# Batch 0's normalised rows transposed by f32 products with an identity, and a new order of the first three batches

## The chip, the core and the metric

One core of a Trainium2 chip. The metric is the device time of one execution in microseconds; a median of several runs is compared. The kernel has one instruction stream per engine: TensorE (PE, matmul), VectorE (DVE), ScalarE (ACT), GpSimd (POOL) and SyncE (SP, which here only issues DMAs). Each stream runs its own list in order, and the lists meet by semaphores.

## What is computed

A pre-norm attention block and a mixture of experts on eight batches of 512 rows of 256, all f32:

```python
x = x + attn(layernorm(x), Wq, Wk, Wv)      # per batch, causal, one head of 256
x = x + ffn(layernorm(x), ...)              # shared expert + top 2 of 8 routed experts
# attn: softmax(mask(q @ k.T) / 16) @ v,  q = x@Wq, k = x@Wk, v = x@Wv
# ffn:  silu(x@gate.T) * (x@up.T) @ down, inner width 512
#       routing: sigmoid(x@router.T + bias), top 2, weights normalised to sum 1
```

The kernel holds each f32 operand of a product as two f16 parts (high and low) and makes three f16 products (high by high, high by low, low by high; PASSES) that accumulate in f32.

## The kernel before

*Numbers.* B = 8 batches of NB = 4 blocks of P = 128 rows, D = 256 = KD * 128 columns. A "low" part is the f32 value minus its high part.

*Stages.* First the constants, wm = Wq Wk^T (`wm_product`, f32 products), the f16 parts of wm, Wv and the router. Then the batches: the first three in an order written out by hand in each engine's list, batches 3 to 7 by `iteration(i)`, which mixes batch i's attention with batch i-2's shared expert. Then the routed experts, in a loop over groups of two pairs of row blocks, whose results are added to the output by indirect DMA.

*A batch.* DVE takes statistics of the rows (`stats_1`, `aggregate_1`), POOL the power (`rstd1`), DVE the shift (`shift_1`). ACT normalises into xn32 (`xn_normalise`, L762) and casts into xnrow (`xn_high`, L736); the low part is made by POOL (`xn_low`, L564), and for batch 0 by DVE (`first_xn_low`, L1124). SP transposes xnrow into xnt by DMA (`xn_transpose`, L321; batch 1's goes to a part of w). Then TensorE makes T = wm applied to xnt (`t_product`, L1811) and V (`v_product`, L1832), the scores (`scores`, L1855, mask added by L1858), and from the transposed exponentials (`p_transpose`, L345, issued by SP) the attention output (`pv`, L1787). ACT evicts high parts (`t_high`, `v_high`, `p_high`, all L736), DVE the low ones (`t_low`, `v_low`, `p_low`, L1124). The second norm's rows go through xrow and a DMA transpose into xn2t (`xn2_transpose`, L336), then `logits` (L1752), `prefix` (the place of each row in its expert, L1764) and the shared expert (`shared_gate_up` L1711, `shared_down` L1725). POOL scatters the rows to DRAM (`scatter`, L605), after `zero_rows` (L613) has filled that tensor.

*Weights.* All expert weights come in 36 pieces of 384 KB through two buffers, wst: SP loads (`w_load`, L311, waits for the low part of the piece two before), ACT scales and casts (`w_scale`, `w_high`, L736), POOL makes the low part (`w_low`, L581). Until the routed experts begin, only the first four pieces are needed by a product.

*The order.* Nothing but the lists and the waits decides it: an engine whose next step waits holds up all behind it. TensorE's first lines before are

```python
wm_product()
t_product(0, 0, 2)
v_product(0, 0, 2)
scores(0, 0, 4)
```

Before `t_product(0, ...)` it waits for xnt_in (the DMA transpose) and wm_lo. The banks are shared: T uses PT0 and PT1, which also hold the scores of blocks 1 and 2; V uses U[0] and U[1], which the shared expert uses too.

## Time and profile before

| | us |
|---|---|
| median of 3 runs | 576.56 (576.01 to 577.16) |
| the profiled execution | 575.5 |
| its span | 573.7 |
| of which TensorE busy | 519.4 |
| span of the three batches written out | 18 to 87 |
| loop over batches 3 to 7 | from 87 on |
| routed experts | 273 to 541 |

The span runs from the first to the last instruction that the profiler saw; 1.8 us of the execution lie around it. TensorE's profile has two rows for a product: PEld is the load of the stationary operand, PE the product. An f32 product appears as two of each. The ends of products are modelled, so the starts are the better guide; a group's time is from the start of its first to the end of its last.

### The profile page before, as it was taken

Reading aid. Unit: us, or ns where it says so; the run is one execution under the profiler, and the core shown is the slowest. Engines: PE = TensorE matmul, PEld = TensorE weight load, DVE = VectorE, ACT = ScalarE, POOL = GpSimd, SP = SyncE. Lnnn points to the kernel's source line nnn. Section 1 sums busy time; section 2 is a strip of 40 time slices with the busy share of each in tenths; the row PEclk is TensorE's granted clock in tenths of the full one; section 3 lists DMA queues with packets and bytes.
Section 4 is the critical chain, followed back from the end, with each engine's and each line's share of the span. In section 5 each row is a group of like instructions: output and inputs, shape, how many; then the busy total and the mean of one; then the engine's idle time right before and its main releaser. Section 6 shows DMA issues by size and latency. Waiting matters only on the chain.

```text
span 573.7 us, 14737 instructions
## 1 busy us (share of the span) xinstructions
PE 519.4 (91%) x4521; PEld 422.1 (74%) x4522; DVE 372.4 (65%) x933; ACT 306.6 (53%) x578; POOL 288.4 (50%) x236
## 2 busy tenths in 40 slices
PE   2778899898989999896999999999999999999980
PEld 1455688686777878775688888788888888888870
DVE  5468999878897978899455455545455554555440
ACT  4979888686767566652243443444444434444440
POOL 3653788676685856766014534434344434344433
PEclk9999999999999999999899999999999999999995
DMA  7898876949493939652636554565655556445542
GB/s 259 219 199 151 155 183 128 256 108 206 134 208 112 201 134 174 178 151 77 139 59 103 82 78 77 84 86 75 90 84 75 82 86 89 76 74 76 82 56 27
DMA packets 147546, 70.45 MB, mean 123 GB/s; under 512 B 122384, under 2 KB 140560, under 8 KB 147504
## 3 DMA queue, kind: packets, MB, share of 16 engines
q1 hardware_dynamic: 133904, 50.69, 42.4%
q0 software_dynamic: 13600, 19.22, 19.3%
q8 instruction: 24, 0.39, 0.3%
q14 instruction: 18, 0.15, 0.1%
HBM read 19.48 MB, written 23.54 MB: 75 GB/s over the span
## 4 chain that ended last, share of the span: by engine, by line
PE 58%; SPq 12%; DMA 10%; DVE 10%; issue 4%; ACT 3%; POOL 2%; POOLq 0%; ACTq 0%; DVEq 0%
PE bank L1711 27%; PE bank L1725 15%; PE bank L1984 6%; SPq L336 4%; DMA wst<-w_all 4%; SPq L345 4%; DMA ptr<-phl 3%; PE bank L1999 3%; SPq L321 2%; PE bank L1832 2%; PE bank L1787 2%; PE bank L1811 2%; PE bank L1855 1%; DMA out<-p,wm 1%; DMA out<-tt,wm 1%
## 5 line engine op out<-in xcount | busy, mean ns | idle before, releaser
L1711 PE MATMUL bank<-xn2t,w 128*128 128x256 f16 x1728 | 197.2, 273 | 0.9 <-DVE th L1298 0.8
L1711 PEld LDWEIGHTS bank<-xn2t,w 128*128 (+1 forms) x1728 | 168.5, 98 | 24.5 <-DVE th L1298 1.4
L691 POOL DMA_INDIRECT out<-p,wm x56 | 87.4, 1561 | 117.1 <-issue 55.0
L1289 DVE SCALAR_TENSOR_TENSOR th<-th,bank 128x512 f32<-128x512 f32 x88 | 60.1, 682 | 71.5 <-ACT th L780 71.4
L1725 PE MATMUL bank<-w,h 128*128 (+1 forms) x864 | 101.3, 273 | 3.0 <-DVE z L1221 2.0
L1725 PEld LDWEIGHTS bank<-w,h 128*128 128x128 f16 x864 | 83.5, 98 | 15.3 <-DVE z L1221 3.2
L736 ACT ACTIVATE h<-th 128x512 f16<-128x512 f32 x72 | 45.2, 628 | 87.0 <-DVE th L1298 85.1
L780 ACT ACTIVATE th<-bank 128x512 f32<-128x512 f32 x88 | 52.4, 596 | 46.9 <-PE bank L1711 46.7
L1124 DVE TENSOR_TENSOR h<-th,h 128x512 f16<-128x512 f32 x72 | 49.8, 692 | 39.2 <-ACT h L736 39.1
L581 POOL TENSOR_TENSOR w<-wst,w 128x768 f16<-128x768 f32 x36 | 59.3, 1649 | 26.3 <-ACT w L736 26.0
L605 POOL DMA_INDIRECT rows<-xrow,sidx x56 | 57.2, 1022 | 27.1 <-DVE sidx L1281 15.3
L1298 DVE SCALAR_TENSOR_TENSOR th<-th,bank 128x512 f32<-128x512 f32 x88 | 60.1, 682 | 2.2
L691 POOL DMA_INDIRECT out<-tt,wm x15 | 24.0, 1597 | 69.8 <-DMA out<-p,wm 39.2
L1984 PE MATMUL bank<-w,ptr 128*128 x180 | 41.3, 379 | 0.0
L1061 ACT ACTIVATE p<-bank,wm 128x256 f32<-128x256 f32 x56 | 23.6, 471 | 23.3 <-issue 13.2
L1787 PE MATMUL bank<-v,ptr 128*128 128x256 f16 x240 | 29.9, 273 | 6.4 <-DMA ptr<-phl 6.4
L736 ACT ACTIVATE wst<-wst 128x768 f32<-128x768 f32 x36 | 29.9, 834 | 8.4 <-DMA wst<-w_all 8.3
L1811 PE MATMUL bank<-xnt,wm 128*128 128x512 f16 x84 | 21.7, 402 | 11.9 <-DVE wm L1125 7.7
L1711 PE MATMUL bank<-w 128*128 128x256 f16 x288 | 32.4, 273 | 0.0
L1787 PEld LDWEIGHTS bank<-v,ptr 128*128 128x128 f16 x240 | 22.3, 98 | 12.2 <-DMA ptr<-phl 9.1
L1984 PEld LDWEIGHTS bank<-w,ptr 128*128 128x128 f16 x180 | 17.6, 98 | 18.2 <-issue 0.3
L736 ACT ACTIVATE w<-wst 128x768 f16<-128x768 f32 x36 | 30.3, 841 | 0.7
(156 smaller groups left out, 710.0 us busy)
## 6 DMA issues: line engine op xcount, KB each, us to landing
wst<-w_all SPq DMA_DIRECT2D x36, 384.0 KB
x<-x SPq DMA_DIRECT2D x8, 512.0 KB, 5.6
out<-x SPq DMA_DIRECT2D x8, 512.0 KB, 4.9
rows<-xrow POOLq DMA_DIRECT2D x1, 1192.5 KB, 7.4
rows<-xrow,sidx POOLq DMA_INDIRECT x56
out<-p,wm POOLq DMA_INDIRECT x56, 4.0
wm<-rows SPq DMA_DIRECT2D x28, 9.0 KB, 1.9
xn2t<-rows SPq DMA_TRANSPOSE x28, 3.7
```

The source lines that it names most:

```text
L581: cc.tensor_tensor(w_ap(j, 1, c * CH, CH), wst[:, (g % 2) * CH:(g % 2 + 1) * CH], w_ap(j, 0, c * CH, CH), ALU.subtract).then_inc(w_lo, 1)
L605: cc.indirect_dma_start(rows, bass.IndirectOffsetOnAxis(ap=sidx_of(b)[:, m:m + 1], axis=0), xrow[b % 2][:, n * RW:(n + 1) * RW].bitcast(I3 ...
L691: cc.indirect_dma_start(out, bass.IndirectOffsetOnAxis(ap=index, axis=0), part, None, compute_op=ALU.add).then_inc(y_out, 16)
L736: return a.activation(o, i, ACT.Copy, scale=scale)
L780: a.activation(th[:, half * 512:(half + 1) * 512], G[half][:, :], ACT.Tanh, scale=0.5 / WS).then_inc(f_tanh, 1)
L1124: return d.tensor_tensor(o, full, hi, ALU.subtract)
L1289: d.scalar_tensor_tensor(out=tb, in0=tb, scalar=1.0, in1=G[half][:, :], op0=ALU.add, op1=ALU.mult).then_inc(f_sg, 1)
L1298: d.scalar_tensor_tensor(out=tb, in0=tb, scalar=0.5 / (WS * WS), in1=U[half][:, :], op0=ALU.mult, op1=ALU.mult).then_inc(f_h, 1)
L1711: ins = mm(dst, w_ap(j, ws, m * MAT + k * I + (2 * half + i) * P, P), moving(ms * KD + k), start=(cnt == 0), stop=(cnt == 3 * KD - 1))
L1725: ins = mm(o[:, a * D:(a + 1) * D], hb[:, (hs * KI + i) * TT + a * P:(hs * KI + i) * TT + (a + 1) * P], w_ap(j, ws, 2 * MAT + i * D, D), s ...
L1787: ins = mm(PV_BANK[q // 2][:, (q % 2) * D:(q % 2 + 1) * D], ptr[:, off + (ps * (q + 1) + kb) * P:off + (ps * (q + 1) + kb + 1) * P], v[:, ...
L1984: ins = mm(o[:, :], xs_t[:, c * P:(c + 1) * P], w_ap(j, ws, m * MAT + kk * I, I), start=(cnt == 0), stop=(cnt == 3 * KD - 1))
```

## The change

Batch 0's normalised rows are no longer cast, split and transposed by DMA. ACT normalises blocks 0 and 1, DVE blocks 2 and 3 (`first_xn_normalise`). TensorE multiplies each 128x128 block of xn32, as the stationary operand, by an f32 identity (`first_transposes`, eight products of 128 columns into PT1 and PT2). ACT casts the two banks into the high half of xnt, DVE subtracts into the low half (`first_xn_high`, `first_xn_low`). The identity is made by POOL in the spare part of w. Batch 0's transpose leaves SP's list, and the counts of xn_lo, xn_hi and xnt_in go down by one batch for all others. The semaphore xn2t_in becomes two, by parity of the batch.

All five lists of the first three batches have a new order. The loop, the tail and the routed experts are as before.

```diff
+        ident32 = spare[:, 4144:4144 + 2 * P].bitcast(F32)
...
+        XN_BANK = (PT1, PT2)
+        xnt4 = xnt[:, :].rearrange("p (n c r) -> p n c r", n=NB, r=P)
...
@@ SP
             x_load(1)
             x_load(2)
+            w_load(0)
             x_load(3)
-            w_load(0)
             w_load(1)
-            xn_transpose(0)
...
             w_load(2)
+            xn_transpose(1)
             w_load(3)
-            xn_transpose(1)
+            x_load(4)
             w_load(4)
-            x_load(4)
             p_transpose(0, 0)
             p_transpose(0, 1)
             p_transpose(0, 2)
-            w_load(5)
             p_transpose(0, 3)
             xn_transpose(2)
+            w_load(5)
             w_load(6)
...
@@ POOL
+            const(cc.memset(ident32, 0.0))
...
+            const(cc.affine_select(out=ident32, in_=ident32, compare_op=ALU.not_equal, fill=1.0,
+                                   base=0, pattern=[[-1, P]], channel_multiplier=1))
...
             rstd1(0)
             rstd1(1)
             w_low(0)
+            xn_low(1)
             w_low(1)
+            w_low(2)
             rstd1(2)
+            xn_low(2)
             zero_rows()
-            xn_low(1)
-            w_low(2)
             w_low(3)
-            xn_low(2)
...
-            scatter(0, 0, 2)
             w_low(8)
-            scatter(0, 2, 5)
+            scatter(0, 0, 5)
             w_low(9)
...
@@ ACT
+            def first_xn_high(k):
+
+                act.wait_ge(xn0_mm, 2)
+                copy(xnt4[:, :, k, :], bank3(XN_BANK[k])).then_inc(xn0_hi, 1)
...
             router_high()
+            xn_normalise(0)
             wv_high()
-            xn_normalise(0)
-            xn_high(0)
+            wm_high()
             w_scale(0)
+            first_xn_high(0)
+            first_xn_high(1)
+            w_scale(1)
             w_high(0)
-            w_scale(1)
-            w_high(1)
-            wm_high()
             xn_normalise(1)
             xn_high(1)
+            v_high(0, 0)
+            t_high(0, 0)
+            t_high(0, 1)
+            w_high(1)
...
@@ DVE
+            def first_xn_normalise():
+
+                dve.wait_ge(shift1, 1)
+                for i in (2, 3):
+                    ins = d.tensor_scalar(xn32[:, i * D:(i + 1) * D], x1[:, i * D:(i + 1) * D], rstd[0][:, i:i + 1],
+                                          nmr[:, i:i + 1], ALU.mult, ALU.add)
+                ins.then_inc(xn0_dve, 1)
+
+            def first_xn_low(k):
+
+                dve.wait_ge(xn0_hi, k + 1)
+                low(xnt4[:, :, KD + k, :], bank3(XN_BANK[k]), xnt4[:, :, k, :]).then_inc(xn0_lo, 1)
...
@@ TensorE
+            def first_transposes(h):
+
+                pe.wait_ge((xn_put, xn0_dve)[h], 1)
+                for n in (2 * h, 2 * h + 1):
+                    for k in range(KD):
+                        ins = mm(XN_BANK[k][:, n * P:(n + 1) * P], xn32[:, n * D + k * P:n * D + (k + 1) * P],
+                                 ident32, start=True, stop=True)
+                ins.then_inc(xn0_mm, 1)
...
             wm_product()
-            t_product(0, 0, 2)
-            v_product(0, 0, 2)
+            first_transposes(0)
+            first_transposes(1)
+            t_product(0, 0, 1)
+            v_product(0, 0, 1)
+            t_product(0, 1, 2)
+            v_product(0, 1, 2)
             scores(0, 0, 4)
+            t_product(1, 0, 1)
             v_product(1, 0, 1)
-            t_product(1, 0, 2)
+            t_product(1, 1, 2)
             pv(0, 0, 1)
             v_product(1, 1, 2)
-            pv(0, 1, 3)
-            scores(1, 0, 2)
+            pv(0, 1, 2)
+            scores(1, 0, 1)
+            pv(0, 2, 3)
+            scores(1, 1, 2)
             pv(0, 3, 4)
             scores(1, 2, 4)
             t_product(2, 0, 2)
-            pv(1, 0, 2)
             v_product(2, 0, 1)
-            pv(1, 2, 4)
+            pv(1, 0, 4)
             v_product(2, 1, 2)
-            scores(2, 0, 3)
+            scores(2, 0, 4)
             logits(0)
             shared_gate_up(0, 0)
-            scores(2, 3, 4)
             prefix(0)
...
```

## Rows read from the trace of the kernel before

**Rows 1.** The page's part 1: busy us, share of the span, instructions.
```profile
PE 519.4 (91%) x4521; PEld 422.1 (74%) x4522; DVE 372.4 (65%) x933; ACT 306.6 (53%) x578; POOL 288.4 (50%) x236
```

**Rows 2.** Windows: stretch, length, then busy us (instructions) of each engine.
```profile
18.00:87.00 69.00, 61.62 (x527) 45.58 (x528) 56.59 (x196) 58.56 (x116) 44.08 (x36) 1.00 0.87 182
87.00:242.00 155.00, 145.40 (x1351) 117.87 (x1349) 133.07 (x405) 109.04 (x213) 106.35 (x91) 1.00 0.71 166
```

**Rows 3.** Timeline, first 19 us: start, length, engine, line, count [idle before, releaser].
```profile
6.34 1.05 POOL L551 TENSOR_TENSOR rstd<-ve,halves 128x4 f32<-128x4 f32 x1 [2.64 <-DVE ve L1144]
6.62 3.78 PE L1688 MATMUL bank<-v 128*128 128x256 f32 x8 [6.62 <-DMA v<-wk_t]
8.47 2.06 ACT L762 ACTIVATE xn<-x,nmr,rstd 128x256 f32<-128x256 f32 x4
12.90 2.04 SPq L321 DMA_TRANSPOSE xnt<-xnrow  x1
16.70 0.58 ACT L736 ACTIVATE wm<-bank 128x512 f16<-128x512 f32 x1
17.31 0.69 DVE L1125 SCALAR_TENSOR_TENSOR wm<-bank,wm 128x512 f16<-128x512 f32 x1 [3.04 <-ACT wm L736]
18.11 0.14 PEld L1811 LDWEIGHTS bank<-xnt,wm 128*128 128x128 f16 x2 [8.43 <-DMA xnt<-xnrow]
18.14 4.37 PE L1811 MATMUL bank<-xnt,wm 128*128 128x512 f16 x12 [7.74 <-DVE wm L1125]
```

**Rows 4.** One line's or tile's instructions, to 40 us: ns min/median/max, first and last start.
```profile
L1688 PEld LDWEIGHTS bank<-v x8: 288/337/337, 6.6 to 9.3; 128*128 128x128 f32 x8
L1811 PEld LDWEIGHTS bank<-xnt,wm x12: 97/147/147, 18.1 to 21.9; 128*128 128x128 f16 x12
```

**Rows 5.** Timeline of TensorE, 18 to 87 us: the products that serve as checkpoints.
```profile
24.96 0.50 PE L1855 MATMUL bank<-xnt,tt 128*128 128x128 f16 x6
...
29.35 1.48 PE L1832 MATMUL bank<-wvs,w 128*128 128x256 f16 x12 [0.74 <-DMA w<-xnrow]
...
40.09 1.48 PE L1787 MATMUL bank<-v,ptr 128*128 128x256 f16 x12 [2.30 <-DMA ptr<-phl]
...
42.74 1.47 PE L1855 MATMUL bank<-w,tt 128*128 128x512 f16 x6
...
45.77 2.75 PE L1811 MATMUL bank<-xnt,wm 128*128 128x512 f16 x12 [1.50 <-DVE w L1124]
...
55.05 0.50 PE L1855 MATMUL bank<-xnt,tt 128*128 128x128 f16 x6
...
58.81 2.78 PE L1711 MATMUL bank<-xn2t,w 128*128 128x256 f16 x24
...
86.66 0.50 PE L1855 MATMUL bank<-xnt,tt 128*128 128x128 f16 x6
```

**Rows 6.** Timeline of DVE and POOL: two DVE steps beside POOL's subtraction.
```profile
32.05 2.13 POOL L564 TENSOR_TENSOR xnrow<-xn,xnrow 128x1024 f16<-128x1024 f32 x1 [2.08 <-ACT xnrow L736]
32.07 2.13 DVE L1144 TENSOR_SCALAR ve<-mv 128x4 f32<-128x4 f32 x1
...
61.20 2.13 POOL L564 TENSOR_TENSOR xnrow<-xn,xnrow 128x1024 f16<-128x1024 f32 x1
61.70 1.65 DVE L1238 CAST idxf<-ix 128x8 f32<-128x8 uint32 x1
```

**Rows 7.** Chain that ended last, two pieces: start, length, what.
```profile
35.09 4.95 DMA ptr<-phl
...
63.87 5.67 DMA xnt<-xnrow
```

**Rows 8.** Groups by line, 18 to 87 us: busy us, mean ns.
```profile
L736 ACT ACTIVATE w<-wst 128x768 f16<-128x768 f32 x11 | 9.2, 838 | 0.1
L581 POOL TENSOR_TENSOR w<-wst,w 128x768 f16<-128x768 f32 x11 | 18.3, 1664 | 4.1 <-ACT w L736 3.9
```

**Rows 9.** Timeline of TensorE at the start of the routed experts.
```profile
273.12 4.87 PE L1725 MATMUL bank<-w,p 128*128 128x256 f16 x24 [5.42 <-DVE p L1124]
```

More of the change, by code:

```diff
@@ L388, in _ @@
             p_transpose(1, 1)
[L389 removed]
             p_transpose(1, 2)
             p_transpose(1, 3)
[L392 removed]
+            w_load(7)
             xn2_transpose(0, 0)
@@ L656, in _ @@
             w_low(11)
+            put_idx(1)
             rstd2(2)
```

251 lines of the change are left out of this document (128 added, 123 removed).

## Prediction

> **What bounds the kernel now.** I read the page's busy shares first, then busy time by stage, then TensorE's timeline, then the other engines only where TensorE waits. The shares [rows 1] name TensorE as the engine to watch (91%). The stages [rows 2] say where it is not full: from 18 to 87 (batches 0 to 2, written out by hand) it works 61.62 of 69 and so idles 7.4, and in the loop over batches 3 to 7 it idles 9.6 in 155. In the first 18 us it works 3.78 [rows 3]. The loop's own order is not edited. So what the change is worth is what it does to the time at which the loop's first product starts, 86.66 us [rows 5], provided that the rest follows rigidly.
>
> What ends the long first wait? Two things, at nearly the same time [rows 3]: the low part of wm (16.70 to 17.28 on ACT, to 18.00 on DVE), and batch 0's DMA transpose, issued 12.90, for which the first weight load waited to 18.11; the first product starts at 18.14. Moving either one alone would give almost nothing. wm is late only because ACT's list puts four weight pieces and batch 0's rows ahead of it: its product had ended at 10.40. The change removes both causes. A second thing to see is the clock: batch 0's twelve 512-column products fill 4.37 us [rows 3], batch 2's twelve 2.75 [rows 5], and of their weight loads most take 147 ns, the fastest, at 21.9, 97 [rows 4]. TensorE is at its lower level (1.2 GHz) there, after 7.7 us of idling, and rises to 2.4 GHz only about 3.8 us into the burst.
>
> **The change, part by part.**
>
> *Constants.* A memset and an affine_select of a 128x128 f32 identity on POOL. The 16-bit ones are 0.2 to 0.3 us; even at twice that, 1.1 us together, they fit in the 2.64 us that POOL idles before the first rstd [rows 3]. Cost nothing; without that cover up to 1.1.
>
> *Normalising batch 0.* ACT does two of four blocks (2.06/2 = 1.03, about 8.05 to 9.1), DVE the other two. A DVE form of this is not in the trace; for 256 columns I bound it by 0.17 (small tensor_scalar) and 0.5 (512 columns take 0.69), done by 8.7. TensorE is in wm's product until 10.40, which hides both.
>
> *The transposes.* Eight f32 products of 128 columns, two records each: 16. From below: wm's eight records of 256 columns took 3.78, half of that per record is 0.236, sixteen make 3.8. From above: a f32 weight load is 337 ns [rows 4]; if it binds, 5.4; if load and product don't overlap at all, 0.337 + 0.213 each, 8.8. At the higher clock throughout about half of the first, 2 us. I take 3.8, because TensorE then runs unbroken from 6.62 on and should rise to the upper level on the way. So the transposes end at 10.4 + 3.8 = 14.2 (range 12.4 to 19.2).
>
> The Trainium skill (TensorE: Matmul & The Clock Gate, "Weight-path perf modes") says fast weight load is off for f32; the trace agrees (337 against 147 ns at the same clock).
>
> *Eviction.* Two ACT copies (0.58, as wm's) and two DVE subtractions (0.69), pipelined: 0.1 + 0.58 + 0.69 + 0.60 + 0.1 = 2.1. First product at 16.3: 1.8 us earlier. wm_low now ends about 12.5 and is no longer a condition. TensorE idles only 2.1 us before it, so I expect the higher clock: another 1.6 us (4.37 less 2.75).
>
> *What this becomes in the new order.* I walked the lists of all engines with the trace's durations: an ACT weight piece 0.84 twice and POOL's part of it 1.66 [rows 8], xn_low 2.13 [rows 6], 512 columns 0.58 on ACT and 0.69 on DVE, less 0.1 where the next follows without a wait; TensorE 1.3 per half product. Checkpoints, before [rows 5] against the walk:
> - scores of batch 0: 24.96 to 22.3. Products end at 21.5, but ACT has two weight halves, batch 1's normalise and cast between: it, not TensorE, sets the 22.3.
> - first product of batch 1: 29.35 to 27.9. Here the gain shrinks to 1.4. Batch 1's rows still go by DMA: cast 19.9, POOL's subtraction 22.1 (in place of 23.8), then 5.3 us to land (12.90 to the load at 18.11; 5.67 later [rows 7]). T's bank is also held until p_low(0,1), about 27.4 to 28.1. TensorE idles 2.2 us where it idled 0.7.
> - last scores of batch 1: 42.74 to 38.9. The P transpose of the last block is issued at 32.1 instead of 35.09, because before a DVE step was stuck 2.13 us [rows 6]; the 2.30 us wait at 40.09 nearly goes.
> - T of batch 2: 45.77 to 42.5, new wait 2.2 (p_low(1,1), and batch 2's transpose beside the 1.2 MB zeroing of the rows, which POOL now issues later).
> - scores of batch 2: 55.05 to 52.1. The P transposes 2 and 3 of batch 1, issued to 45.6, bind.
> - shared gate/up 0: 58.81 to 56.9, with 1.3 us of scores done ahead: 3.2 in all.
> - then the prefix stands right behind gate/up half 0 and waits for the router's mask, about 1.8 us; before, scores of block 3 stood between.
> - from there TensorE is nearly full: the loop starts at 84.3 against 86.66.
> Sum: 1.8 (start) + 1.6 (clock) - 1.0 (net new idle) = 2.4. The walk leaves out small semaphore gaps; I take 2.2.
>
> *Moved steps.* On SP, w_load(0) passes x_load(3): the first piece comes sooner, the fourth x is needed at 29. One transpose issue (2.04) is gone. w_load(5) and (7) come after the P transposes: the pieces are used by ACT at 42.6 and 50.5, half a dozen us later than they can land. On POOL, scatter(0) takes five in a row ahead of w_low(9), some 6 us, which only delays weights that the loop's list takes later. put_idx(1) is 0.2. On ACT and DVE the reordered steps are in the walk. Splitting xn2's semaphore costs nothing: each consumer waits for the same landing.
>
> **What can take it back.** In the trace a DVE step on SBUF data that starts while POOL runs ends with POOL's instruction: 2.13 beside 2.13, and the cast of the router's indices 1.65 [rows 6]. Aggregates, bias rows and casts meet other POOL steps in the new order; the walk has two such meetings, 1.5 and 1.1 us. The Trainium skill (SBUF — State Buffer, on the shared port pair) calls this an exclusive lock for the whole instruction; the trace agrees. Which meetings occur can't be read from the lists to 0.1 us. Further on, the loop's waits are on transposes and DVE, and TensorE's 5.42 us wait before 273.12 [rows 9] ends with DVE's table: all of these move with the start, each worth some tenths either way.
>
> **Rivals.**
> 1. *Absorbed.* Two more meetings of DVE and POOL on the chain, or 1.5 us more at the mask. For: DVE is busy 56.6 of 69 us in this stage [rows 2]. Against: the old order had them too. Left: 0 to 1.1 us; about 575.9.
> 2. *The clock stays low through batch 0's products.* They end about 1.9 us later, 23.6, T's low half about 24.9, scores 25.0, so 2.7 of the gain go: 576.9. For: the gap of 2.1 us, and f32 products of 128 columns may leave the array half idle. Against: the idle stretch of 2.30 us before 40.09 is followed by full-speed products (1.48 for twelve of 256 columns) [rows 5].
> The Trainium skill (TensorE: Matmul & The Clock Gate, "Part 4: PE-mode transpose") says that the upper clock doesn't engage for transpose-mode products. These are plain f32 products, so I don't expect it to apply; by it the time would be this rival's. No row here shows such products.
> 3. *Slower: the transposes don't overlap their weight loads.* 8.8 us, ending 19.2: the whole chain over ACT starts 5.0 later, so 2.2 becomes -2.8: 579.4. It decides from 0.38 us a record (6.0 us in all, end at 16.4) on; slower by 0.2% from 0.45. For: 337 ns loads ahead of products of only 128 columns, eight different blocks. Against: in wm's product [rows 3] eight records of 634 ns fill 3.78 us, so they do overlap.
> 4. *More.* The order removes idle time that my walk still has (2.2 and 2.2 before T of batches 1 and 2, 1.8 at the mask) and the transposes run at the upper clock: 4.2 us, 572.4.
>
> **The numbers.** The profiled execution took 575.5 (span 573.7 and 1.8 around it); the median of the runs is 576.56, 1.06 above it. 575.5 - 2.2 = 573.3, on the scale of the median 574.4. About 0.2% (1.15 us) is what a measurement of this kernel can tell from no change. Forecast (gain 1.15 to 3.4): 0.42, its own range 573.2 to 575.4. More: 0.13. Absorbed: 0.20. Low clock: 0.10. Slower: 0.15. Faster 0.55, same 0.30, slower 0.15. The range leaves out most of the slower case and the far end of the fourth: 572.2 to 577.6.
>
> **What would show it.** In the profile after: f32 products of 128 columns between 10.4 and about 14.2; first 512-column product at about 16.3 with 97 ns weight loads; scores of batch 0 at 22.3, first product of batch 1 at 27.9 released by the DMA or DVE's p; last scores of batch 1 near 39; T of batch 2 near 42.5; a wait for the mask of 1 to 2 us; loop from 84.3, and 31 us an iteration as before. The prediction is wrong if the transposes take over 6 us, if batch 1's transposed rows land after 29.3, or if the loop starts early and the end doesn't move with it.

## The result: slower by 0.7 %

The changed kernel took 580.87 us (median of 4 runs, 580.49 to 582.48) beside 576.28 us for the kernel before (median of 4, 575.52 to 577.16): 1.0072 times, 95 % interval 1.0041 to 1.0103. Forecast were 574.4 us and "faster". Two later measurements, on other chips, gave 1.0091 (1.0052 to 1.0129) and 1.0069 (1.0041 to 1.0096). The profiled execution took 582.48 us, its span was 580.6 us, against 575.5 and 573.7. It is the slowest of its four and the one before is the fastest of its four, so the two spans differ by 6.9 us where the medians differ by 4.6.

First the page of the profile after, part 1 (busy us, share of the span, instructions), as [rows 1].

```profile
span 580.6 us, 14775 instructions
PE 524.4 (90%) x4537; PEld 426.2 (73%) x4538; DVE 376.6 (65%) x936; ACT 305.1 (53%) x577; POOL 289.2 (50%) x238
```

TensorE's work grew by 5.0 us, of which the transposes are 2.2; the products are otherwise the same ones. Two groups alone, T of batch 2 and gate/up 0, took 3.9 us more below, at the lower clock, and T of batch 0 took 1.4 us less. The windows of the changed kernel show where (stretch, length, busy us of PE, PEld, DVE, ACT and POOL with their instructions, PEclk, DMA share, GB/s), as [rows 2].

```profile
0.00:18.00 18.00, 8.65 (x44) 6.80 (x46) 9.80 (x35) 8.74 (x16) 6.46 (x23) 1.00 0.65 212
18.00:87.00 69.00, 55.55 (x455) 40.31 (x454) 55.09 (x180) 52.54 (x108) 40.64 (x32) 0.93 0.84 171
87.00:242.00 155.00, 145.80 (x1359) 118.71 (x1357) 133.34 (x406) 110.51 (x213) 104.77 (x91) 1.00 0.70 166
```

From 18 to 87 us TensorE works 55.55 us where it worked 61.62, and its mean clock is 0.93. From 87 to 242 us it is as busy as it was (145.80 against 145.40). So most of the result lies ahead of the loop; the table has the share. TensorE's timeline after, at the checkpoints of [rows 3] and [rows 5]:

```profile
10.21 2.16 PE L1750 MATMUL bank<-w,xn 128*128 128x128 f32 x16
15.08 1.47 PE L1850 MATMUL bank<-xnt,wm 128*128 128x512 f16 x6 [2.71 <-DVE xnt L1144]
...
21.67 0.51 PE L1895 MATMUL bank<-xnt,tt 128*128 128x128 f16 x6 [1.21 <-DVE tt L1144]
...
27.22 1.46 PE L1850 MATMUL bank<-w,wm 128*128 128x512 f16 x6 [1.89 <-DVE w L1144]
...
41.22 1.47 PE L1895 MATMUL bank<-w,tt 128*128 128x512 f16 x6 [1.66 <-DVE x L1410]
45.36 4.14 PE L1850 MATMUL bank<-xnt,wm 128*128 128x512 f16 x12 [2.62 <-DMA xnt<-xnrow]
...
55.23 0.50 PE L1895 MATMUL bank<-xnt,tt 128*128 128x128 f16 x6
...
62.98 5.28 PE L1740 MATMUL bank<-xn2t,w 128*128 128x256 f16 x24 [3.52 <-DVE v L1144]
68.05 0.23 PE L1802 MATMUL bank<-mask,tri 128*128 128x32 f16 x1
...
92.23 0.50 PE L1895 MATMUL bank<-xnt,tt 128*128 128x128 f16 x6
```

| first product of | before [rows 3, 5] | forecast | after | after less before |
|---|---|---|---|---|
| T of batch 0 | 18.14 | 16.3 | 15.08 | -3.1 |
| scores of batch 0 | 24.96 | 22.3 | 21.67 | -3.3 |
| batch 1 (before V, after T) | 29.35 | 27.9 | 27.22 | -2.1 |
| last scores of batch 1 | 42.74 | 38.9 | 41.22 | -1.5 |
| T of batch 2 | 45.77 | 42.5 | 45.36 | -0.4 |
| scores of batch 2 | 55.05 | 52.1 | 55.23 | +0.2 |
| shared gate/up 0 | 58.81 | 56.9 | 62.98 | +4.2 |
| loop | 86.66 | 84.3 | 92.23 | +5.6 |

The part of the change that is its point worked better than forecast: 3.3 us were gained by 21.67. Then they were lost: 1.2 us up to batch 1, as forecast, 2.3 between there and the scores of batch 2, 4.0 more up to gate/up 0, and 1.4 on the way to the loop. Of the 4.0, 1.3 us are not lost time but the scores of block 3, which stood behind gate/up 0 before and stand ahead of it now; so the stretch from there to the loop loses 2.7 us and not 1.4, and 2.5 of these are the slow gate/up products themselves (5.28 us against 2.78). From the loop's first scores to the end of the span are 487.0 us before and 488.4 after, so 1.4 of the 6.9 us of span come behind the loop's start.

### The profile page after: what moved, and what is told of

It is laid out like the page before. It is cut to its first block, busy times and chain, and to the rows that moved or that the text cites. A ratio compares the mean times of both kernels' runs of the same rounds, so it can differ in the third digit from the quotient of the medians.

```text
span 580.6 us, 14775 instructions
## 1 busy us (share of the span) xinstructions
PE 524.4 (90%) x4537; PEld 426.2 (73%) x4538; DVE 376.6 (65%) x936; ACT 305.1 (53%) x577; POOL 289.2 (50%) x238
## 4 chain that ended last, share of the span: by engine, by line
PE 54%; SPq 12%; DMA 11%; DVE 9%; issue 5%; ACT 4%; POOL 3%; POOLq 0%; ACTq 0%; DVEq 0%
PE bank L1740 26%; PE bank L1763 14%; PE bank L2032 6%; DMA wst<-w_all 5%; SPq L344 4%; DMA ptr<-phl 4%; SPq L353 4%; PE bank L2047 3%; SPq L329 2%; PE bank L1872 1%; DMA out<-tt,wm 1%; DMA out<-p,wm 1%; DVE th L1327 1%; PE bank L1825 1%; SPq L319 1%
## 5 line engine op out<-in xcount | busy, mean ns | idle before, releaser
L1740 PE MATMUL bank<-xn2t,w 128*128 128x256 f16 x1728 | 200.0, 275 | 4.6 <-DVE v L1144 3.5
L703 POOL DMA_INDIRECT out<-tt,wm x15 | 25.2, 1679 | 71.4 <-DMA out<-p,wm 40.5
L1825 PEld LDWEIGHTS bank<-v,ptr 128*128 128x128 f16 x240 | 22.4, 98 | 11.5 <-DMA ptr<-phl 7.3
L1740 PEld LDWEIGHTS bank<-w 128*128 128x128 f16 x288 | 27.9, 98 | 3.7
## 6 DMA issues: line engine op xcount, KB each, us to landing
rows<-xrow POOLq DMA_DIRECT2D x1, 1192.5 KB, 10.5
```

What stands on the lines that cost most here:

```text
L703: cc.indirect_dma_start(out, bass.IndirectOffsetOnAxis(ap=index, axis=0), part, None, compute_op=ALU.add).then_inc(y_out, 16)
L1740: ins = mm(dst, w_ap(j, ws, m * MAT + k * I + (2 * half + i) * P, P), moving(ms * KD + k), start=(cnt == 0), stop=(cnt == 3 * KD - 1))
L1825: ins = mm(PV_BANK[q // 2][:, (q % 2) * D:(q % 2 + 1) * D], ptr[:, off + (ps * (q + 1) + kb) * P:off + (ps * (q + 1) + kb + 1) * P], v[:, ...
```

## Where the start was lost, read from the trace after

**Between 34 and 45 us.** DVE, POOL and SP's queue, in that order (start, length, engine, line, operation, count):

```profile
36.79 2.81 DVE L1164 TENSOR_SCALAR ve<-mv 128x4 f32<-128x4 f32 x1
```

```profile
35.01 1.28 POOL L626 DMA_DIRECT2D rows<-xrow  x1
36.32 3.25 POOL L594 TENSOR_TENSOR w<-wst,w 128x768 f16<-128x768 f32 x2
```

```profile
35.16 2.29 SPq L329 DMA_TRANSPOSE xnt<-xnrow  x1
38.00 2.36 SPq L319 DMA_DIRECT2D wst<-w_all  x2
```

A four-element step of DVE, ve of batch 3, takes 2.81 us (0.17 when POOL is idle): it starts while POOL splits two weight pieces back to back (36.32 to 39.57), and ends with the second. Behind it stand the row maximum of the next scores and the additions that free TensorE's bank, so TensorE waits 1.66 us at 41.22. At the same time POOL issues the 1.2 MB zeroing of the rows 0.15 us before SP issues batch 2's transpose. The transposed rows are used at 45.36, 10.2 us after their issue; in [rows 3] batch 0's took 5.2. In the view of DMA issues (KB each, median us to landing) the zeroing takes 10.5 us to land; it was 7.4 before:

```profile
rows<-xrow POOLq DMA_DIRECT2D x1, 1192.5 KB, 10.5
```

**Between 57 and 68 us.** The timeline of ACT, then POOL, then DVE:

```profile
54.72 0.84 ACT L748 ACTIVATE wst<-wst 128x768 f32<-128x768 f32 x1 [1.27 <-DMA wst<-w_all]
55.47 2.06 ACT L776 ACTIVATE xn<-x,nmr,rstd 128x256 f32<-128x256 f32 x4
```

```profile
57.68 1.98 POOL L564 TENSOR_TENSOR rstd<-ve,halves 128x4 f32<-128x4 f32 x2 [2.37 <-ACT xn L776]
59.64 2.11 POOL L577 TENSOR_TENSOR xnrow<-xn,xnrow 128x1024 f16<-128x1024 f32 x1
```

```profile
58.72 0.16 DVE L1169 SCALAR_TENSOR_TENSOR nmr<-mv,rstd 128x4 f32<-128x4 f32 x1 [0.95 <-POOL rstd L564]
...
59.70 2.08 DVE L1169 SCALAR_TENSOR_TENSOR nmr<-mv,rstd 128x4 f32<-128x4 f32 x1 [0.75 <-POOL rstd L564]
...
62.16 0.67 DVE L1144 TENSOR_TENSOR v<-bank,v 128x512 f16<-128x512 f32 x1
...
65.39 1.22 DVE L1267 CAST idxf<-ix 128x8 f32<-128x8 uint32 x1
...
66.90 0.19 DVE L1271 TENSOR_TENSOR mask<-one_hot 128x32 f16<-128x32 f32 x1
```

ACT waits 1.27 us for a weight piece, so its normalising of batch 3 ends at 57.5; POOL's rstd of batch 4 has to wait for that and holds rstd of batch 1's second norm behind it; both shifts of DVE wait for POOL (0.95 and 0.75), and the second, a step of 0.16 us, then lies 2.08 us beside POOL's subtraction. v_low(2,0), which frees the bank of gate/up 0, stood ahead of all this in the old order and stands behind it in the new one. TensorE idles 3.52 us and then runs its 24 products in 5.28 us instead of 2.78. Windows of 1 us of the same stretch (stretch, length, PE, PEld, DVE, ACT, POOL, PEclk, DMA share, GB/s):

```profile
62.00:63.00 1.00, 0.02 (x1) 0.05 (x2) 1.00 (x5) 1.00 (x3) 0.00 (x0) 0.50 0.00 1
...
67.00:68.00 1.00, 1.00 (x6) 0.75 (x5) 1.00 (x3) 0.94 (x2) 0.98 (x1) 0.50 0.48 99
68.00:69.00 1.00, 1.00 (x13) 0.79 (x11) 0.90 (x8) 0.70 (x2) 0.15 (x1) 0.67 0.40 60
```

So a chain of waits can be read. Whether each of them costs what it seems to is another question; the rest of this section's reading was put to the chip.

## Experiments

The experiments ran on other chips than the result, and the kernel before took 577.8 to 582.8 us there; so ratios are compared, each with the kernel before measured beside it. The scatter is larger than in the first measurement, and intervals of about ±0.3 % are what it allows. Between groups of measurements ratios carry over roughly: the changed kernel had 1.0069 to 1.0091 in three, the transposes alone 1.0047 and 1.0080 in two. One group is to be read with more care. On one and the same chip (14) the kernel before took 577.75 us beside new_order_dma, front_new and score_shift and 582.78 beside after_third, 0.9 % more, while the variants had medians of 585.7 to 587.7 us in the first group and 586.1 to 589.4 in the second. The three ratios of 1.015 and above are all of the first group, which had no changed kernel in it, and may owe a part of that to the kernel before.

### One wait at a time

`v_first`: v_low(2,0) ahead of the waiting shifts.

```diff
             row_max(2, 1)
-            shift_1(4)
             minus_max(2, 1)
+            v_low(2, 0)
+            shift_1(4)
             shift_2(1)
             row_max(2, 2)
-            v_low(2, 0)
```

> One line of DVE's list moved: batch 2's V subtraction stands before shift_1(4) and shift_2(1) instead of behind them. Theory A (the 3.52 us wait ahead of the first gate/up product, and the clock that falls after it): the wait goes, the 24 products take 2.8 us instead of 5.3, the loop starts 4 to 6 us earlier than 92.2, time 575 to 577. Rival B (something else is late just behind it, a transpose or the mask): the wait moves to the prefix or to T of batch 3 and the loop starts less than 2 us earlier, time above 579. Rival C (the loss sits in the loop or the tail, not here): the loop starts earlier and the time stays at 581.

`filler`: thirty products whose result nobody reads, to keep TensorE busy in its wait.

```diff
             logits(0)
+            filler(30)
             shared_gate_up(0, 0)
```

> The changed kernel plus 30 products of 256 columns into a bank that the next product overwrites, put into the wait ahead of the first gate/up product (their results are not used). The wait stays as long as it was. If half of the loss there is the clock, the 24 gate/up products take 2.8 us instead of 5.3 and the time is about 2.5 us below 580.9, 578.4. If the slow products have another cause (operands, memory), they stay at 5.3 us and the time stays at 581 or above.

`agg_early`: the DVE step that got stuck for 2.81 us goes elsewhere.

```diff
             v_low(0, 1)
+            aggregate_1(3)
             p_low(0, 3)
...
-            aggregate_1(3)
```

> One line of DVE's list moved: aggregate_1(3) stands before p_low(0,3), where POOL is idle, instead of where POOL makes two weight pieces. Theory A: its 2.81 us step shrinks to 0.17, the last scores of batch 1 start at about 39.5 instead of 41.2, but T of batch 2 waits for its DMA transpose (45.3) anyway, so the time moves by less than 1 us. Rival: the stuck step delays everything behind it on DVE and the gain of 2 us or more reaches the loop, time 579 or less.

`zero_early`: the zeroing ahead of batch 2's rows.

```diff
             rstd1(2)
+            zero_rows()
             xn_low(2)
-            zero_rows()
```

> One line of POOL's list moved: the 1.2 MB zeroing of the rows is issued before batch 2's subtraction (at about 26.5, where POOL idles 6.6 us) instead of just behind it, so it no longer runs beside batch 2's DMA transpose. Theory A: the transpose takes 5 to 6 us instead of 10, T of batch 2 starts at about 43.5 instead of 45.4 and at the upper clock (2.8 us instead of 4.1), but batch 0's P transposes get later by 1 to 3 us; net 0 to 3 us faster than 580.9. Rival: the transpose's 10 us have another cause (weight loads in the same queue), T of batch 2 still starts after 45, time 581 or more.

| kernel | ratio (95 %) | T of batch 2: start, length, wait | gate/up 0 | loop |
|---|---|---|---|---|
| the change, result | 1.0072 (1.0041 to 1.0103) | 45.36, 4.14, 2.62 for the transpose | 62.98, 5.28, 3.52 for DVE | 92.23 |
| the change, after_again | 1.0091 (1.0052 to 1.0129) | 46.74, 4.45, 2.77 for the transpose | 63.16, 2.78, 2.00 for DVE | 95.89 |
| the change, after_third | 1.0069 (1.0041 to 1.0096) | 48.68, 4.45, 3.55 for the transpose | 65.11, 4.45, 2.02 for DVE | 98.89 |
| v_first | 1.0096 (1.0063 to 1.0129) | 48.36, 4.45, 3.25 for DVE | 62.63, 2.78, no wait | 94.57 |
| filler | 1.0090 (1.0057 to 1.0123) | 47.69, 4.23 | 65.23, 2.78 | 95.32 |
| agg_early | 1.0104 (1.0046 to 1.0162) | 48.57, 5.30, 5.90 for the transpose | 65.91, 2.78, 2.00 for DVE | 98.17 |
| zero_early | 1.0088 (1.0055 to 1.0120) | 49.05, 4.44, 2.09 for DVE | 66.69, 4.45, 3.25 for DVE | 96.96 |

The first three rows are one and the same kernel: its own profiles differ by 3.3 us at T of batch 2 and by 6.7 at the loop, so that starts of single profiles can't be compared to a us or two; which wait is there and which isn't can. None of the four variants is faster than the change by more than the error. Each took away what it was meant to and met the next: v_first has no wait at gate/up 0, and 3.62 us at the prefix, for the mask; agg_early has no stuck step, and 5.90 us for the DMA transpose that ran beside the zeroing; zero_early let that transpose land in time and put the zeroing beside the transposes of batch 0's P. In filler gate/up 0 ran at full speed (2.78) and the ratio stayed; but it ran at full speed in after_again too, without any filler, behind a wait of 2.00 us. So filler shows that a full clock at gate/up 0 doesn't bring the time back, and not that the filler is what kept it.

### Several, and the parts alone

`after_again` is the changed kernel once more, as it is. `shift_late` takes both shifts out of each other's way; `three_moves` adds agg_early and zero_early.

```diff
-            rstd1(4)
             rstd2(1)
+            rstd1(4)
             xn_low(3)
...
             row_max(2, 1)
-            shift_1(4)
             minus_max(2, 1)
...
             ffn_low(0, 1)
+            shift_1(4)
             p_low(2, 3)
```

> The changed kernel unaltered, so that the variants sent with it have it on the same chip. 0.7 to 1.0% above the kernel before, with the waits of its first profile: about 3.5 us before the first gate/up product and slow products behind it.

> The changed kernel with batch 4's shift put back behind ffn_low(0,1) on DVE and batch 1's second rstd put back ahead of batch 4's on POOL. v_first showed that the wait only moved from the first gate/up product to the mask, so DVE is what is late there. Theory D (DVE is held up some 3.6 us between 58 and 62 by waiting for two rstd and by 2.0 us of nmr stuck beside xn_low(3)): both the wait before gate/up and the one before the prefix shrink to under 1.5 us, the products run at the upper clock, the loop starts 4 us or more earlier, 3 to 5 us faster than after_again. Rival (DVE is simply full, the order of these two steps doesn't matter): under 1 us faster.

> shift_late with the moves of agg_early and zero_early as well. Alone, each of the two only uncovered the other: with the aggregate early T of batch 2 waited 5.9 us for its DMA transpose, with the zeroing early it waited for p_low(1,1) behind the stuck aggregate. If they are one wait with two holders, both together start T of batch 2 about 2 us earlier than after_again, at the upper clock, and the time is 1 to 3 us below shift_late. If a third thing holds it, it equals shift_late within 0.5 us.

Measured: after_again 1.0091 (1.0052 to 1.0129), shift_late 1.0081 (1.0048 to 1.0115), three_moves 1.0075 (1.0044 to 1.0107). The ratio of after_again was as expected, the wait was not: 2.00 us before gate/up 0 and full speed behind it, where 3.5 us and slow products were expected. None of the three can be told from the others by its time. In shift_late gate/up 0 starts at 59.62 without a wait, 3.4 us earlier than in the result, but the loop at 93.06. TensorE's timeline of shift_late, and DVE's:

```profile
65.41 0.19 PE L1802 MATMUL bank<-mask,tri 128*128 128x32 f16 x1 [3.01 <-DVE mask L1271]
...
66.10 4.13 PE L1740 MATMUL bank<-xn2t,w 128*128 128x256 f16 x24 [0.38 <-DVE v L1144]
```

```profile
60.54 0.79 DVE L1257 TENSOR_SCALAR pr<-ez 128x32 f32<-128x32 f32 x1
...
62.84 1.15 DVE L1267 CAST idxf<-ix 128x8 f32<-128x8 uint32 x1
64.03 1.10 DVE L1269 TENSOR_TENSOR one_hot<-eidx,idxf 128x64 f32<-128x64 f32 x1
65.16 0.19 DVE L1271 TENSOR_TENSOR mask<-one_hot 128x32 f16<-128x32 f32 x1
```

The wait has gone one place on, to the mask, whose chain on DVE meets POOL three times (0.16 to 0.23 us of work each where POOL is idle), and with the wait the clock falls there (4.13).

`transposes_old_order`, twice, the second as `transposes_again`: the products with the identity, with the lists of the kernel before on all engines, except that on ACT xn_normalise(0) stands ahead of wv_high, wm_high behind it, and the copies of batch 0's rows behind w_scale(0), and that on DVE wm_low stands ahead of the copies' low parts. `new_order_dma` is the converse: the new lists, with batch 0's rows cast, split and transposed by DMA as before.

> The f32 transposes alone: all lists in the old order but for the steps that they need (wm's high part right behind its product, the two evictions, batch 0's transpose gone from SP). Theory D (the loss is the new order's, the transposes gain): first product at 15 to 15.5, loop start 84 to 86 against 86.7, 0 to 3 us faster than the kernel before. Rival E (the early start itself costs, because every later step is bound by DMA and DVE, which gain nothing): the loop starts at 86.7 or later, time equal to before or slower.

> The transposes alone in the old lists once more (transposes_old_order), beside the kernel before and after on one chip. Theory: by themselves they start TensorE 1.5 us earlier and the rest takes it back, ratio 1.000 to 1.005; if it is again 1.004 to 1.006 with an interval above 1.001, the transposes too cost something (scores of batch 0 wait for ACT's copy of T behind four weight pieces: 4 us in the first run).

> The new order alone: the lists of the changed kernel, but batch 0's rows go by the DMA transpose as before (cast on ACT, low part on DVE, issue on SP behind w_load(1)). Theory 'the new order is what costs': the first product at about 18, checkpoints to 43 about 1 to 2 us later than in the changed kernel, and at the loop nearly as late: 587 to 588, ratio 1.009 to 1.011. Rival 'the transposes cost as much as the order': ratio 1.004, 584 to 585.

Measured: transposes alone 1.0047 (1.0012 to 1.0081) and 1.0080 (1.0049 to 1.0110); new order alone 1.0149 (1.0117 to 1.0182). Against the kernel before measured beside it, the order alone costs, clearly, and more than its theory said (1.009 to 1.011). Whether it costs more than order and transposes together (1.0069 to 1.0091) is not clear: by its median (585.68 us, against 586.49 for after_third on the same chip) new_order_dma is no slower. The transposes alone cost too, as rival E had it (loop at 93.23 and 91.25, not at 84 to 86), and TensorE's timeline of transposes_again shows where the first of it is lost:

```profile
10.05 2.65 PE L1753 MATMUL bank<-w,xn 128*128 128x128 f32 x16
16.06 5.30 PE L1853 MATMUL bank<-xnt,wm 128*128 128x512 f16 x12 [3.36 <-DVE xnt L1145]
...
27.18 0.51 PE L1898 MATMUL bank<-xnt,tt 128*128 128x128 f16 x6 [2.94 <-DVE tt L1145]
```

T's products end at 21.4 and ACT has copied both halves by 24.2; DVE is what is late, as its timeline and POOL's show:

```profile
21.05 4.88 DVE L1170 SCALAR_TENSOR_TENSOR nmr<-mv,rstd 128x4 f32<-128x4 f32 x1
25.85 1.27 DVE L1145 TENSOR_TENSOR tt<-bank,tt 128x512 f16<-128x512 f32 x2
```

```profile
20.86 1.28 POOL L626 DMA_DIRECT2D rows<-xrow  x1
22.17 2.14 POOL L577 TENSOR_TENSOR xnrow<-xn,xnrow 128x1024 f16<-128x1024 f32 x1
24.26 1.63 POOL L594 TENSOR_TENSOR w<-wst,w 128x768 f16<-128x768 f32 x1
```

A step of 0.15 us is held for 4.88 us, from POOL's issue of the zeroing through two further instructions, until POOL pauses at 25.89; in transposes_old_order it is held for 4.88 us as well. In before_again, the kernel before on the same chip, the same step starts 0.14 us into the same issue and is through in 0.14:

```profile
20.76 0.14 DVE L1149 SCALAR_TENSOR_TENSOR nmr<-mv,rstd 128x4 f32<-128x4 f32 x1
```

Here it starts 0.19 us into it. This meeting puts the scores of batch 0 at 27.18, not at 25.73 as in before_again (below), and the 1.5 us are still there at gate/up 0 (60.59 against 59.10). It is 2.3 us at T of batch 3, for whose transpose TensorE waits 1.49 us against 0.72, and 3.2 at the loop (91.25 against 88.07), so about half of the lateness comes later. No run took the meeting away by itself; its price of 1.5 us is a reading of two profiles on one chip.

### The new front on the old rest

`before_again` is the kernel before, profiled beside these. `front_new` has the new lists up to the last scores of batch 1 and the old ones from T of batch 2 on, but with the zeroing ahead of xn_low(2). `score_shift` is shift_late with the scores of block 3 back ahead of the prefix.

```diff
-            scores(2, 0, 4)
+            scores(2, 0, 3)
             logits(0)
             shared_gate_up(0, 0)
+            scores(2, 3, 4)
             prefix(0)
```

> The kernel before, unchanged, as the yardstick: a profile of it taken on the same chip as the others. Expected about 582 us, ratio 1.000. The theories use its checkpoints: T of batch 2 at about 45.8, shared gate/up 0 at 58.8, loop start at 86.7, each perhaps 0.5 to 1 us later than in the first profile.

> The changed kernel up to the last scores of batch 1 (transposes by products, new lists of all five engines, but the zeroing of the rows ahead of xn_low of batch 2 and the aggregate of batch 3 early, as before), and from T of batch 2 on every engine's list as in the kernel before. Theory 'the gain is made in batches 0 and 1 and lost between 43 and 69 by the new order there': last scores of batch 1 some 1 to 1.5 us earlier than before, gate/up 0 at about 57 to 58 and the loop 1 to 2 us earlier than in the kernel before: 580 to 581, ratio 0.997 to 0.999. Rival 'whatever starts early waits later, because DVE and the transposes set the pace from 30 on': the loop starts where it did, ratio 1.000 +/- 0.002. Rival 'the new front itself costs something later (weights later, the clock)': like the changed kernel, 586 to 587, ratio 1.008.

> The changed kernel with shift_late's two moves (shift_1(4) behind ffn_low(0,1) on DVE, rstd2(1) ahead of rstd1(4) on POOL) and with scores(2,3) behind gate/up half 0, ahead of the prefix, as in the kernel before. Theory 'the prefix's wait for the mask (3.0 us in shift_late) and the fall of the clock behind it are the loss once gate/up is on time': the wait shrinks by the 1.3 us of scores and the second half of gate/up runs at 2.78 instead of 4.1 to 4.5: loop 1.5 to 2.8 us earlier than in shift_late, 585, ratio 1.003 to 1.005. Rival 'DVE's and the transposes' pace sets the loop's start': the wait only moves to the scores or the later products, ratio 1.008.

Measured: before_again 1.0022 (0.9999 to 1.0046), which is the same kernel on both sides, so 0.2 % is what such a ratio can be off by, loop at 88.07; score_shift 1.0150 (1.0121 to 1.0178), and the prefix still waits 3.23 us for the mask although 1.4 us of scores stand in front of it; front_new 1.0178 (1.0140 to 1.0216), the highest ratio of all. That is what the third rival of front_new's expectation says, and score_shift lies above both of its theories. My theory for front_new was wrong as the kernel was made, and ACT's and SP's timelines show the mistake:

```profile
46.25 0.84 ACT L749 ACTIVATE wst<-wst 128x768 f32<-128x768 f32 x1 [8.25 <-DMA wst<-w_all]
```

```profile
31.18 5.26 SPq L353 DMA_TRANSPOSE ptr<-phl  x2
...
40.29 1.94 SPq L329 DMA_TRANSPOSE xnt<-xnrow  x1
```

The zeroing, issued at 28.18, ran beside batch 0's P transposes (two issues take 5.26 us; TensorE waited 3.71 us for one of them), and w_load(5) stood behind batch 2's transpose in SP's queue, so ACT, whose list was the old one there, idled 8.25 us. A joint between lists has to fit on five engines at once.

> The changed kernel, unchanged, as the yardstick for the other three on the same chip. Expected 1.008 to 1.015 times the kernel before (585 to 587 us).

> The changed kernel with the zeroing store issued by POOL right behind w_low(0), at about 18 us, and aggregate_1(3) ahead of p_low(0,3). Theory (a), the zeroing's place is the loss: no DMA transpose behind batch 1's rows runs beside it, batch 2's rows land in 5 us instead of 10, T of batch 2 starts at 43 to 44 (45.4 to 46.7 in the changed kernel), the loop 2 to 4 us earlier, ratio 1.002 to 1.006. Rival (b), the lists from batch 2 on: T of batch 2 earlier, but gate/up 0 or the prefix wait that much longer, loop no more than 1 us earlier than in the changed kernel. Third: batch 1's own transposes are the ones that now run beside it, first product of batch 1 at 31 instead of 27 to 28, and nothing is gained.

> New front up to batch 1's last scores, the old lists from T of batch 2 on (as front_new), with front_new's two faults mended: the zeroing store at about 18 us instead of 28, and w_load(5) ahead of the last P transpose as in the kernel before. Theory: the 8.3 us wait of ACT for weights and the 3.7 us of TensorE for P go, and the early start is kept: loop 1 us earlier to 1 us later than in the kernel before, ratio 0.998 to 1.003. Rival, the front's gain can't be carried past 45 whatever the lists: 1.005 or more.

Measured: after_third 1.0069 (1.0041 to 1.0096), zero18_agg 1.0106 (1.0059 to 1.0152), front_mended 1.0099 (1.0070 to 1.0128). Zeroing at 18 us frees batch 2's transpose (T of batch 2 at 44.88, 48.68 in after_third) but now runs beside batch 1's, whose first product waits 3.12 us (28.41): the third case of its expectation. In front_mended w_load(5), ahead of the last P transpose, waits in SP's queue for POOL's third weight piece, which the new front finishes only at 39.6; the P transpose behind it is issued at 39.98 and TensorE waits 4.63 us for it. The two theories stayed undecided, but after_third showed the size of the first suspect: ve of batch 3 starts in POOL's issue of the zeroing, at 37.62, and is held to 41.99, where the second of the two weight pieces behind it ends.

```profile
37.62 4.37 DVE L1164 TENSOR_SCALAR ve<-mv 128x4 f32<-128x4 f32 x1
```

It was 2.81 us in the profile of the result, 2.60 in shift_late, 4.12 in after_again, 4.37 in new_order_dma and 4.38 in score_shift. The kernels whose aggregate_1(3) or zeroing is elsewhere (three_moves, zero18_agg, zero13_all, front_new, front_good) have no held step above 2.1 us.

`zero13_all`: the changed kernel with the zeroing where no transpose is on its way, and the moves of agg_early and shift_late. `front_good`: the new lists of all engines up to about 45 us (DVE's up to the scores of batch 1), with that zeroing and aggregate_1(3) moved likewise; from there the old lists.

```diff
             rstd1(1)
+            zero_rows()
             w_low(0)
...
             xn_low(2)
-            zero_rows()
             w_low(3)
```

> The changed kernel with three waits taken away together: the zeroing store at about 13 us, aggregate_1(3) ahead of p_low(0,3) on DVE, and shift_1(4) behind ffn_low(0,1) with rstd2(1) ahead of rstd1(4). Theory, these three are the loss: T of batch 2 at 43 to 45, gate/up 0 at 57 to 59, and the mask's wait of 1.5 to 3 us is what remains: loop at 89 to 90.5, ratio 1.003 to 1.005. Rival, DVE's and POOL's meetings in the mask's chain take it back: loop at 92 to 94 as in shift_late and three_moves, ratio 1.007 to 1.010.

> New front up to batch 1's last scores with its own weight loads and ACT steps, the zeroing store issued at about 13 us (before w_low(0)), aggregate_1(3) ahead of p_low(0,3), and the old lists of PE, DVE, POOL and ACT from T of batch 2 on. Theory, the lists of batch 2 lose the gain: scores of batch 1 at 35 to 36, T of batch 2 at 43 to 44.5, gate/up 0 at 57 to 59, loop 0.5 to 2 us earlier than in the kernel before (85 to 87.5), ratio 0.997 to 1.000. Rival, the gain of the front can't be carried whatever the lists, because ACT's weight pieces that the front puts off come due there: loop at 89 or later, ratio 1.004 or more.

Measured together: **zero13_all 583.01 us, 1.0012 (0.9985 to 1.0040)**; **front_good 579.97 us, 0.9955 (0.9931 to 0.9979)**, beside 581.88 us for the kernel before. front_good beats both kernels. Its time is better than its theory said (0.997 to 1.000) although its loop starts later (88.72 against 85 to 87.5), and the same goes for zero13_all (1.003 to 1.005; loop at 89 to 90.5). TensorE's timeline of front_good, then POOL's and the landing of the zeroing:

```profile
15.95 2.74 PE L1853 MATMUL bank<-xnt,wm 128*128 128x512 f16 x6 [3.07 <-DVE xnt L1145]
...
43.95 2.75 PE L1853 MATMUL bank<-xnt,wm 128*128 128x512 f16 x12 [1.50 <-DVE w L1145]
...
57.66 2.78 PE L1743 MATMUL bank<-xn2t,w 128*128 128x256 f16 x24
...
63.45 0.19 PE L1805 MATMUL bank<-mask,tri 128*128 128x32 f16 x1 [1.66 <-DVE mask L1272]
...
63.59 5.40 PE L1743 MATMUL bank<-xn2t,w 128*128 128x256 f16 x48
```

```profile
13.43 1.28 POOL L626 DMA_DIRECT2D rows<-xrow  x1
```

```profile
rows<-xrow POOLq DMA_DIRECT2D x1, 1192.5 KB, 7.7
```

T of batch 2 runs at 43.95 in 2.75 us, gate/up 0 at 57.66 in 2.78, and no wait of TensorE between 34 and 70 us exceeds 1.7 us. In zero13_all gate/up 0 is as early (58.03), and the mask's wait of 3.01 us, with 4.41 us for the half product behind it, remains: its loop starts at 91.31, front_good's at 88.72.

**What follows.** zero13_all, the changed kernel without the three waits that were read from the trace, is as fast as the kernel before (1.0012), while the changed kernel had 1.0069 to 1.0091. That is about 0.6 %, but between groups of measurements: the changed kernel was not measured beside zero13_all. So the three moves together probably remove most of the loss; how much each of them does is not shown. The place of the zeroing on POOL is common to most of the waits: it lengthens transposes, and POOL's run of instructions behind it holds DVE. three_moves and zero13_all differ in nothing but that place (27 against 13 us) and measured 1.0075 and 1.0012, again on different chips. A rival stands untested: that the zeroing at 13 us would do it alone. It was tried at 27 (zero_early) and at 18 (zero18_agg), each time beside other transposes, and never at 13 without the other moves.

The new order from there on costs 3.0 us more (583.01 less 579.97, same chip, measured together). front_good as a whole gains 1.9 us on the kernel before by the medians, 2.6 by the ratio. How much of that is the transposes by products is not shown: front_good also has the zeroing 7 us earlier and new lists for the first two batches, and neither the kernel before with the early zeroing nor front_good with batch 0's rows by DMA was measured. Open too is in which stretch front_good keeps its gain. Its profile, one execution on another chip than before_again's, has gate/up 0 at 57.66 against 59.10 but the loop at 88.72 against 88.07; the times, not the two profiles, show the gain.

## Why the prediction was wrong, step by step

- *Constants, normalising on DVE: right.* DVE's two blocks took 0.73 us, within the 0.34 to 1.0 given.
- *Transposes: over-sized, in the safe direction.* 16 records in 2.16 us, not 3.8 (1.95 to 3.17 in the other runs). The rate of the wm product, 0.236 us for 128 columns, didn't carry over. Rival 3 (8.8 us) was far off.
- *Eviction and first product: right.* 2.71 us of idle against 2.1, start at 15.08 against 16.3. The clock held in this profile (1.47 us for six products). In others with the same first products it didn't, and the length of the idle stretch doesn't sort them: 2.74 us for the six after 2.27 (filler), 2.65 (score_shift), 2.79 (zero13_all), 2.97 (after_third) and 3.07 (front_good), but 1.47 after 2.73 (zero18_agg) and 1.51 after 3.70 (after_again). So "TensorE idles only 2.1 us before it, so I expect the higher clock" came true by luck as much as by reason. Rival 2 thus comes and goes. What it costs at the scores of batch 0 runs from next to nothing (21.77 in zero13_all against 21.64 in zero18_agg) to 2.7 us (24.35 in front_good against 21.67), and front_good has none of it left at the last scores of batch 1 (40.92 against 41.22). The price on record for this rival is also mis-added: 574.4 and 2.7 are 577.1, not 576.9. The Trainium skill (TensorE: Matmul & The Clock Gate, "Part 4: PE-mode transpose") says the upper clock doesn't engage for transpose-mode products; behind these plain f32 products the next six took 1.47 us, which is the upper level, so nothing of the kind is seen for them in the result, and no run here has transpose-mode products.
- *The clock in the first 20 us is read from lengths.* The prediction puts TensorE at the lower level at 18.14 in the kernel before, by 4.37 us for twelve products and 147 ns weight loads. The granted clock of the same stretch reads 1.00 in the profile before, from 18 to 23 us. The two don't agree, and the lengths are what the prediction's reading rests on.
- *Batch 1: right up to 28 us* (27.22 against 27.9, wait 1.89 against 2.2), *then wrong.* "Last scores at 38.9" failed on the size of one term: the meetings of DVE with POOL. The walk had two, of 1.5 and 1.1 us. The real ones ahead of the loop are 1.27, 2.81, 2.08, 1.22 and 1.25 us, and the second is over 4 us in later runs: a step is held until POOL pauses, not until its instruction ends, so 1.65 or 2.13 [rows 6] is no upper bound. The prediction said itself that these meetings can't be read from the lists; the consequence, a wider range upward, was not drawn. By the last scores of batch 1 the forecast was missed by 2.3 us. The held step is about 1.4 of what was missed: from the first scores of batch 0 to the last of batch 1 the result takes 19.55 us, agg_early and zero13_all without that step 18.05 and 18.16, the walk 16.6. Which step took the rest is not shown. The Trainium skill (SBUF — State Buffer, "Who interferes with whom") has the lock for a whole instruction; the holds of 2.81 to 4.88 us, over two and three instructions, are longer than that.
- *T of batch 2 at 42.5: wrong by 2.9 us.* The zeroing was named, but priced inside a 2.2 us wait, with 5.3 us for the transpose. Beside the zeroing it took 10.2. And the clock fell in the 2.62 us wait (4.14 instead of 2.75). I had argued against that from one row: full speed behind 2.30 us of idling [rows 5]. That is no bound: in after_third the clock fell behind 2.02 us (gate/up 0, 4.45).
- *Gate/up 0 at 56.9: wrong by 6.1 us, the largest miss.* The dependence was left out of the walk: rstd of batch 4 waits for ACT's normalising of batch 3, holds the next rstd behind it on POOL, and shift_1(4), moved from behind ffn_low(0,1) to ahead of v_low(2,0), hands that wait to TensorE. The prediction says of the reordered steps that they "are in the walk"; a step moved forward past an important one needs its own release time looked up. This is the step of the prediction that failed by most: the path from the scores of batch 2 to gate/up 0 was walked without that wait (3.52 us) and without the lower clock behind it (2.5 us), and the loop came 7.9 us later than forecast. shift_late confirms the dependence: with both steps moved back gate/up 0 starts without a wait. That alone didn't bring the time back (1.0081).
- *Prefix waits 1.8 us for the mask:* none in the result (the lateness fell on gate/up 0), 3.01 to 3.62 us once that was mended. Right in kind.
- *SP's moves: half right.* The weight pieces were to be used "half a dozen us later than they can land"; that fails for w_load(5) and w_load(7): ACT waited 1.24 and 1.27 us for pieces.
- *The loop is rigid: right for this pair, not in general.* +5.6 us at its start, +5.8 at the routed experts (278.94 against 273.12 [rows 9]), +6.9 in the span. But over all twenty profiles, on several chips, the time from the loop's first scores to the end runs from 486.7 us (score_shift) to 494.6 (front_mended). That is as much as the whole effect, so the loop's start in one profile is a weak forecast of the time. No run here shows what makes this difference.
- *The rivals.* What happened is the first one's mechanism (more meetings of DVE and POOL on the chain), at three times its size; it was capped at "no gain" without a reason why it should stop there. The slower case was given only to the transposes. A gain of 2.2 us won in the first 20 us of a stage in which DVE is busy 56 of 69 us should have had a slower rival among the lists.

## What to carry to other kernels

A faster step at the head of a hand-written schedule is worth what the order behind it lets through; here kernels with the same transposes were 0.5 to 0.8 % slower with the old lists, 0.7 to 0.9 % slower with the new ones and 0.45 % faster with a joint of both and the zeroing early. When lists are rearranged, look up for every step that moves ahead of a bank-freeing one when its own release comes, for every large store which transposes run beside it, and for every small DVE step how long POOL's unbroken run is there. When waits are removed one by one and nothing changes, it doesn't show that they are harmless: remove them together. And measure the unchanged kernel with every group: its own profiles differed by more here than most of what was tried.

## What the hardware showed that I had not expected

- A small DVE step on SBUF can be held through several POOL instructions that follow one another closely, a DMA issue of 1.28 us among them: 2.81, 4.37 and 4.88 us. Entering that issue 0.13 or 0.14 us after its start (before, before_again) or 0.18 or 0.19 us (transposes_old_order, transposes_again) made the difference between 0.14 and 4.88 us. Not every step is held: in the profile of the result the four statistics of 1.40 us at 48.53 and the index searches of 0.16 us at 65.00 ran at their usual length beside POOL's weight pieces.
- The 1.2 MB store lands in 7.3 to 7.7 us when it is issued at 13 or at 20 to 22 us, in 8.5 to 9.5 at 18 us or at 27 to 28, where it meets batch 1's transpose or batch 0's P transposes, and in 10.5 to 11.5 from 35 us on, beside batch 2's transpose; that transpose takes 10.2 us instead of 5.2, and two P transposes take 5.26 us to issue (front_new) instead of 2.59 (the result, at 46.74).
- TensorE's granted clock fell to 0.50 after most idle stretches of 2.02 to 3.55 us, in before_again after one of 1.60 (gate/up 0, 4.22 us), and stayed at 1.00 after others of 2.00 (after_again) and 2.73 (zero18_agg). In after_again it read 1.00 up to 17 us, through 3.70 us of idling and the six products behind it (1.51 us), and 0.50 from there on while TensorE was working.
- f32 products of 128 columns with f32 weights run in 2.16 us for 16 records behind other f32 products, faster per record than half of a 256-column one (0.135 against 0.236 us); in other runs of the same products it was 0.122 to 0.198.
